# Message-passing kernel: node table ahead of the radial rows, rows broadcast from DRAM in nine pieces, first pass without a barrier

## What is computed

```python
s_j = silu(x[src][:, 384:] @ W1 + b1) @ W3 + b3
rbf = sqrt(2 / R_CUT) * sin(n * pi * r / R_CUT) / r      # n = 1..20, one r for each edge
edge_basis = (rbf * cutoff(r)) @ W2 + b2                 # 384 wide
s1, s2, s3 = thirds of s_j * edge_basis
msg = [v_j * s1 + s3 * edge_attr, s2]                    # 512 wide
x = x + segment_sum(msg, dst)
# a second round: U, V, norms and a gate on x[src], summed by dst again
out = layernorm(x0 + x)
```

## Time and profile before

| | |
|---|---|
| median of three runs | 798.62 us |
| the profiled execution's own span, first to last instruction | 711.8 us |
| DVE busy | 537.0 us (75%) |
| PE busy | 505.8 us (71%) |
| ACT busy | 389.5 us (55%) |
| POOL busy | 370.2 us (52%) |
| DMA: moved, mean rate | 139.26 MB, 196 GB/s |
| first pair's product in the pass (L926) | 154.72 us |
| last pair's product | 549.95 us |

### The profile page before, as it was taken

One profiled execution on the slowest core, in us unless ns is written; L12 is line 12 of the kernel. 1 busy time (PEld: TensorE's weight loads), 2 busy tenths in 40 slices (PEclk: granted clock), 3 DMA queues, 4 the chain that ended last, 5 costly groups with the idle time before them and its releaser, 6 DMA issues.

```text
span 711.8 us, 13058 instructions
## 1 busy us (share of the span) xinstructions
PE 505.8 (71%) x4260; PEld 234.1 (33%) x4269; DVE 537.0 (75%) x1192; ACT 389.5 (55%) x713; POOL 370.2 (52%) x375
## 2 busy tenths in 40 slices
PE   0276430038888888888888888888888286689996
PEld 0232110013333333334433333333333153344443
DVE  8868861029999999999999999999999443354283
ACT  1054331046777777776776777777776364343200
POOL 5004440067777777777777777777773131025300
PEclk9975555559999999999999999999999688689999
DMA  8413777699888888898888888888884400000021
GB/s 277 166 21 99 199 229 222 183 256 306 269 269 272 269 275 270 267 275 268 269 273 269 270 271 271 270 270 269 273 271 149 160 3 0 1 0 1 2 89 56
DMA packets 54193, 139.26 MB, mean 196 GB/s; under 512 B 10366, under 2 KB 21850, under 8 KB 54124
## 3 DMA queue, kind: packets, MB, share of 16 engines
q0 software_dynamic: 25120, 102.91, 46.3%
q1 hardware_dynamic: 23132, 25.80, 12.8%
q10 hardware_dynamic: 5872, 9.68, 4.1%
HBM read 120.47 MB, written 17.54 MB: 194 GB/s over the span
## 4 chain that ended last, share of the span: by engine, by line
DVE 39%; PE 35%; DMA 8%; issue 8%; ACT 3%; SPq 2%; POOL 2%; DVEq 1%; ACTq 1%; POOLq 0%
PE psum L1192 11%; DVE side L929 10%; PE psum L1282 9%; DVE hot L920 5%; DMA part_rows<-side 5%; DVE side L926 4%; PE psum L1157 4%; DVE work L929 3%; DVE work L947 3%; PE psum L1186 3%; PE psum L1251 3%; DVE hot L911 2%; SPq L358 2%; DVE side L916 2%; DMA side<-node_table,src_c 2%
## 5 line engine op out<-in xcount | busy, mean ns | idle before, releaser
L486 POOL DMA_INDIRECT side<-node_table,src_c x234 | 224.4, 959 | 71.3 <-issue 60.4
L604 ACT ACTIVATE side<-key_no,less_key 128x320 bf16<-128x320 f32 x314 | 159.3, 557 | 30.7 <-SPq L384 28.9
L612 ACT ACTIVATE side<-side,one_f 128x640 bf16<-128x640 bf16 x157 | 128.1, 816 | 10.0 <-PE psum L1168 10.0
L1157 PE MATMUL psum<-w2s,radial 123*128 123x384 bf16 x314 | 78.7, 333 | 66.3 <-DVE side L929 43.5
L1186 PE MATMUL psum<-side,hot 128*32 128x512 f32 x468 | 123.1, 605 | 0.5 <-DVE side L929 0.5
L929 DVE TENSOR_TENSOR side<-side,psum 128x768 f32<-128x768 f32 x117 | 110.5, 945 | 0.0
L486 POOL DMA_INDIRECT work<-node_table,src_c x80 | 76.8, 960 | 60.6 <-SPq L384 36.5
L1192 PE MATMUL psum<-side,hot 128*32 128x128 f32 x1404 | 99.4, 277 | 0.0
L926 DVE TENSOR_TENSOR side<-side,psum 128x512 f32<-128x512 f32 x117 | 79.4, 678 | 1.3 <-DMA side<-node_table,src_c 1.3
L1168 PE MATMUL psum<-side 128*128 128x320 bf16 x314 | 70.3, 306 | 0.5 <-ACT side L612 0.5
L1192 PEld LDWEIGHTS psum<-side,hot 128*32 128x32 f32 x1404 | 68.0, 109 | 0.1
(11 more groups left out here) (202 smaller groups left out, 738.0 us busy)
## 6 DMA issues: line engine op xcount, KB each, us to landing
radial<-part_rows SPq DMA_DIRECT2D x36, 270.0 KB
part_rows<-side SPq DMA_DIRECT2D x6, 810.0 KB, 12.7
side<-node_table,src_c POOLq DMA_INDIRECT x234, 4.2
sum_rows<-stage SPq DMA_DIRECT2D x212, 16.0 KB
node_table<-work ACTq DMA_DIRECT2D x10, 320.0 KB, 7.6
sum_rows<-zeros_bf SPq DMA_DIRECT2D x1, 2688.0 KB, 18.8
side<-sum_rows ACTq DMA_DIRECT2D x10, 256.0 KB, 4.7
xw<-in_x ACTq DMA_DIRECT2D x1, 2304.0 KB
```

What stands on the lines that cost most here:

```text
L486: g.indirect_dma_start(out=rows[i % SLOT_PAIRS][:, j, :], out_offset=None, in_=node_table, in_offset=bass.IndirectOffsetOnAxis(ap=src_c[:, ...
L604: a.activation(key_off[:, b, j, :], key_no[:, :], ACT.Abs, bias=less_key[:, t:t + 1]).then_inc(L["key_off_made"], 1)
L612: a.activation(key_hot[:, b, :, :], key_off[:, b, :, :], ACT.Relu, bias=one_f[:, :], scale=-1.0).then_inc(L["key_hot_made"], 1)
L1157: last = mm(bank[2 * (i % 2) + j][:, 0:C3], radial[0:RROWS + 3, t * P:(t + 1) * P], w2s[:, :], start=True, stop=True)
```

## The change

- **Order.** x is loaded into an area of its own (`x_in`), the 128 scalar columns first. Sigmoid, filters and the node table come before the radial pieces; the table has four buffers (`TABLES`), and its ten DVE products stand between the edge-table steps. The split of W2 and the biases moves from DVE to POOL, the copies of the edge attributes to ACT.
- **Radial rows.** r and `coef` are stored in DRAM as f32, and each piece's 120 rows of either are read back by one transfer that repeats each chunk 20 times (`rc_piece`, 360 KB). `pick`, the bf16 parts and PE's spreading are gone. Nine pieces of 768 columns, three `wave` buffers, still two of parts. DVE subtracts for pieces 0 to 3, POOL for 4 to 8, after it has issued the gathers of pairs 0 to 7.
- **SP's order.** Parts of piece 0 are stored, then the zeros of `sum_rows` are written (2688 KB; before this was at the start), then piece 0 is loaded; pieces 1 to 8 are all stored, then all loaded (48 transfers), then x is loaded a second time into `xw` for the residual (2304 KB and a tail), and only then come the stores of the sums.
- **First pass.** `message_pass`, `sum_pass`, `key_pass`, `gather` and `store_sums` run once outside a loop, each engine behind its own waits and without `pass_go`; further passes stand behind an `If` that this data does not take. DVE starts its pass when all nine pieces are scaled. In `take_total` the wait is now for `L["stored"]` at `64 * (n - 1)`: the same condition.

```diff
-PIECES = 6
-PB = 3
+PIECES = 9
+WAVES = 3
+POOL_FROM = 4
+TABLES = 4
...
-            sp.wait_ge(S["dve_const"], 2)
-            sp.dma_start(sum_rows.rearrange("(p b r) c -> p b (r c)", p=P, b=ZB),
-                         zeros_bf[:, :].bitcast(F32).unsqueeze(1).to_broadcast((P, ZB, 256))).then_inc(S["sums_zeroed"], 16)
...
+            sp.wait_ge(S["ld_r"], 32)
+            sp.dma_start(rc_rows[0].rearrange("(g f) -> g f", f=GE), r_r).then_inc(S["r_stored"], 16)
...
+            def store_parts(i):
+                sp.wait_ge(S["lo_made"], i + 1)
+                sp.dma_start(part_rows[:, :, i * PC:(i + 1) * PC].rearrange("k p f -> p k f"), part[i % 2]
+                             ).then_inc(parts_stored[i % 2], 16)
...
+            sp.wait_ge(S["r_stored"], 16)
+            for i in range(2):
+                sp.dma_start(r_in[i], rc_piece(0, i)).then_inc(r_loaded[i], 16)
+            sp.wait_ge(S["rc_made"], 1)
+            sp.dma_start(rc_rows[1].rearrange("(g f) -> g f", f=GE), coef).then_inc(S["coef_stored"], 16)
...
-                sp.wait_ge(S["lo_made"], i + 1)
-                sp.dma_start(part_rows[:, :, i * PC:(i + 1) * PC].rearrange("k p f -> p k f"), part[:, i % 2, :, :]
-                             ).then_inc(parts_stored[i % 2], 16)
-                if i:
-                    load_stack(i - 1)
-            load_stack(PIECES - 1)
-            sp.wait_ge(S["ranges_set"], 1)
-            stored_reg = sp.alloc_register("sums_stored")
-            sp.reg_mov(stored_reg, 0)
+                store_parts(i)
+                if i == 0:
+                    sp.dma_start(sum_rows.rearrange("(p b r) c -> p b (r c)", p=P, b=ZB),
+                                 zeros_bf[:, :].bitcast(F32).unsqueeze(1).to_broadcast((P, ZB, 256))).then_inc(S["sums_zeroed"], 16)
+                    load_stack(0)
+            for i in range(1, PIECES):
+                load_stack(i)
...
-                        sp.wait_ge(stored, sp.snap(stored_reg))
-                        sp.sem_inc(S["stores_seen"], 1)
+                        sp.wait_ge(L["stored"], 64 * n)
...
+            sp.dma_start(xw[:, 0:NFULL, :], x[0:NFULL * P, :].rearrange("(w p) f -> p w f", p=P)).then_inc(S["ld_x"], 16)
+            sp.wait_ge(S["x_pads"], 2)
+            sp.dma_start(xw[0:NTAIL, NFULL, :], x[NFULL * P:N, :]).then_inc(S["ld_x"], 16)
+            store_sums()
...
+            pool.wait_ge(S["edges_taken"], 3)
+            for b in range(TABLES):
+                pool.wait_ge(table_stored[b], 16 * through(NW, b, TABLES))
+            for i in range(SLOT_PAIRS):
+                gather(i)
+            for i in range(POOL_FROM, PIECES):
+                wv, pt = wave[i % WAVES], part[i % 2]
                 pool.wait_ge(S["hi_made"], i + 1)
-                g.tensor_tensor(wave[:, b, :], wave[:, b, :], part[:, b, 0, :], ALU.subtract).then_inc(S["wave_less_hi"], 1)
+                pool.wait_ge(S["lo_made"], POOL_FROM)
+                g.tensor_tensor(wv, wv, pt[:, 0, :], ALU.subtract).then_inc(S["wave_less_hi"], 1)
                 pool.wait_ge(S["mid_made"], i + 1)
-                g.tensor_tensor(part[:, b, 2, :], wave[:, b, :], part[:, b, 1, :], ALU.subtract).then_inc(S["lo_made"], 1)
...
+                g.tensor_tensor(pt[:, 2, :], wv, pt[:, 1, :], ALU.subtract).then_inc(S["lo_made"], 1)
+            for i in range(SLOT_PAIRS, PAIRS):
+                gather(i)
+            with more_passes(pool), pool.Fori(0, EXTRA) as r:
...
+            act.wait_ge(S["x_pads"], 1)
+            load_x(C3, D, S["ld_s"])
+            for to, from_ in ((w1[:, :], W1), (b1c[:, :], b1.rearrange("(p a) -> p a", a=1)), (w3[:, :], W3)):
+                a.dma_start(to, from_).then_inc(S["ld_table_weights"], 16)
+            load_x(0, C3, S["ld_v"])
...
+                       bank[(2, 3, 4)[c]][:, 0:NCOL].rearrange("p (j g) -> p j g", j=TJ)).then_inc(S["attr_taken"], 1)
 
             def take_filter(w):
-                b = w % 2
+                b = w % TABLES
                 act.wait_ge(S["filter_made"], w + 1)
-                if w >= 2:
-                    act.wait_ge(table_stored[b], 16 * (w // 2))
-                    act.wait_ge(S["table_vec_made"], w - 1)
-                a.copy(first_filter[:, b, :], bank[6 + b][:, 0:C]).then_inc(S["filter_taken"], 1)
-                a.copy(table_out[:, b, C3:TW], bank[6 + b][:, C:C3]).then_inc(S["table_rest_made"], 1)
+                if w >= TABLES:
+                    act.wait_ge(table_stored[b], 16 * (w // TABLES))
+                a.copy(table_out[:, b, C3:TW], filter_bank(w)[:, C:C3]).then_inc(S["table_rest_made"], 1)
 
             def store_table(w):
                 act.wait_ge(S["table_vec_made"], w + 1)
                 act.wait_ge(S["table_rest_made"], w + 1)
-                a.dma_start(node_table[w * P:(w + 1) * P, :], table_out[:, w % 2, :]).then_inc(table_stored[w % 2], 16)
...
+
+            def sine(i):
+                act.wait_ge(S["turn_made"], i + 1)
+                a.activation(wave[i % WAVES], wave[i % WAVES], ACT.Sin, scale=TWO_PI).then_inc(S["sin_done"], 1)
+
+            def high_part(i):
+                act.wait_ge(S["wave_scaled"], i + 1)
+                if i >= 2:
+                    act.wait_ge(parts_stored[i % 2], 16 * (i // 2))
+                a.copy(part[i % 2][:, 0, :], wave[i % WAVES]).then_inc(S["hi_made"], 1)
+
+            def middle_part(i):
                 act.wait_ge(S["wave_less_hi"], i + 1)
-                a.copy(part[:, i % 2, 1, :], wave[:, i % 2, :]).then_inc(S["mid_made"], 1)
-
-            for i in range(PIECES + 1):
-                b = i % 2
-                if i + 1 < PIECES:
-                    load_piece(i + 1, 0)
+                a.copy(part[i % 2][:, 1, :], wave[i % WAVES]).then_inc(S["mid_made"], 1)
+
+            for i in range(PIECES + 2):
                 if i >= 2:
-                    middle(i - 2)
-                    for w in (2 * i - 4, 2 * i - 3):
-                        if w < NW:
...
+            act.wait_ge(S["dve_const"], 7)
             act.wait_ge(S["tables_made"], 4)
 
             def key_offsets(i):
@@ -612,9 +600,6 @@
...
+            def turns(i):
+                wv = wave[i % WAVES]
+                dve.wait_ge(r_loaded[i % 2], 16 * (i // 2 + 1))
+                if i >= WAVES:
+                    dve.wait_ge(S["lo_made"], i - WAVES + 1)
+                v.tensor_scalar(wv, r_in[i % 2], harmonic[:, :], None, ALU.mult).then_inc(S["turn_begun"], 1)
+                dve.wait_ge(S["turn_begun"], i + 1)
+                v.tensor_scalar(nearest, wv, MAGIC, MAGIC, ALU.add, ALU.subtract).then_inc(S["turn_near"], 1)
+
+            def remainder(i):
+                wv = wave[i % WAVES]
...
+                dve.wait_ge(coef_loaded[i % 2], 16 * (i // 2 + 1))
+                v.tensor_tensor(wv, wv, coef_in[i % 2], ALU.mult).then_inc(S["wave_scaled"], 1)
+
+            def less_high(i):
+                wv = wave[i % WAVES]
+                dve.wait_ge(S["hi_made"], i + 1)
+                v.tensor_tensor(wv, wv, part[i % 2][:, 0, :], ALU.subtract).then_inc(S["wave_less_hi"], 1)
+
+            def low_part(i):
+                dve.wait_ge(S["mid_made"], i + 1)
+                v.tensor_tensor(part[i % 2][:, 2, :], wave[i % WAVES], part[i % 2][:, 1, :], ALU.subtract
+                                ).then_inc(S["lo_made"], 1)
+
             for i in range(PIECES + 1):
...
-
-            def messages(i):
+                    turns(i)
+                if 2 <= i < POOL_FROM + 2:
+                    less_high(i - 2)
+                if i < PIECES:
+                    remainder(i)
+                if 2 <= i < POOL_FROM + 2:
+                    low_part(i - 2)
+                if i:
+                    scaled(i - 1)
+                if i == 1:
+                    dve.wait_ge(S["uv_turned"], 1)
+                    v.tensor_copy(uT, bank[6][:, 0:C]).then_inc(S["uv_taken"], 1)
+                elif i == 2:
+                    dve.wait_ge(S["uv_made"], 1)
+                    v.tensor_copy(u_uv[:, 1, :], bank[7][:, 0:C]).then_inc(S["uv_set"], 1)
+
...
+            message_pass()
...
+            def sum_pass():
...
+            sum_pass()
+            with more_passes(pe), pe.Fori(0, EXTRA) as r:
+                pe.wait_ge(L["counts_taken"], NG)
...
```

586 lines of the change are left out of this document (273 added, 313 removed).

## The result

The changed kernel takes 826.92 us in the median of four runs (822.58 to 834.95), beside 798.18 us (796.58 to 803.75) for the kernel before: a ratio of 1.0339, interval 1.0286 to 1.0392. It is slower, by 28.7 us between the medians. The ratio leaves out one run, of 834.95 us, that counts as slow; over the other three the difference is 27.2 us. The forecast was 814.0 us with a range of 780 to 836, and slower was its likeliest case.

A forecast was written before the change was run, and what follows sets the result against it. It took DVE at 2.52 us a pair, with POOL at 2.5, to leave the pass no slack. Span 711.8 + 14 (later end) + 1 (restart) = 727 us; with 87 us carried over, 814 us, range 780 to 836.

The forecast's parts named there:

- The mechanism: Near pair 13: first sums queue behind SP's loads and x, `take_total` waits, a hole of 25 to 50 us on four engines.
- The way from ACT to the rest: At pair 13: its keys wait behind `take_total` on ACT, then PE's count, DVE's one-hots and POOL's slots, so the pass stops.
- Set-up to the first piece: Before the pieces: DVE begins its first piece at 46 us, bounds 40 and 52; before 45.62.
- The pieces: Nine-piece set-up: first low part near 58 us, `high_part(3)` at 94, last low part at 125, bounds 110 and 136.
- a rival: Piece set-up: broadcast loads and DVE stalled beside POOL push the low part to 136 us or later; 825 to 840, chance 0.08.
- Start of the pass: First pass: pair 2's product at 128 us against 161.39, 33 us gained, bounds 20 and 48.
- The loads and what stands behind them: SP's queue from 125 us: 48 loads 49 us, x 7, sums some 3, beside gathers of 26; landing 184 to 210.
- The landing of the first sums: First group's store at 202 us; pair 13 near 203.5 against 189.53 before, so the pass ends 14 us later.
- The 87 us: Difference between the profiled span and the median time of the kernel before, carried over unchanged to the forecast time.
- The pass: Main loop over pairs: no slack at 2.52 us a pair; unrolling costed at 0, at best -12 us.
- (a): Likeliest case: loads go into the pass and hold ACT; end 5 to 31 us later, 804 to 830, likeliest 814; chance 0.52.
- (c): Faster: first sums reach DRAM before ACT needs them at 156 us, or nearly; 766, or 770 to 790; chance 0.17.

The follow-up runs named there:

- e4: Changed kernel with SP loading only pieces 1 to 3 before the sums, 30 loads and x's second load on ACT's queue in the key pass; 716.46 us, ratio 1.002.
- e9: As e4, but SP loads piece 1 alone before the sums and 42 loads are on ACT's queue from pair 6; 791.9 us, ratio 0.9804.
- e6: Changed kernel with the five loads of U, V, Wu1, bu1 and Wu2 on SP behind the stores of pieces 1 to 3; 754.21 us, ratio 1.0535.
- e8: Changed kernel with piece 0's loads moved behind the store of piece 3 and the zeros behind that of piece 6 on SP; 820.39 us, ratio 1.0182.
- a0: Changed kernel, nothing edited, on a chip where the kernel before takes 715.5 us; 753.33 us, ratio 1.0541.
- e10: As e7, but the weight loads behind the stores of pieces 0 to 2 and DVE's two copies in steps 6 and 7; 685.59 us, ratio 0.9561.
- e2: Changed kernel with the zeros of sum_rows written early, ahead of the pieces; 752.22 us, ratio 1.0494.
- b0: Kernel before, nothing edited, profiled a second time; 721.69 us, span 719.9.
- e7: e8 and e9 together on the changed kernel, with the five weight loads on SP behind the stores of pieces 4 to 6; 780.73 us, ratio 0.9651.

## Why the prediction was right, and where it was not

**The mechanism was right.** Slower came from where it was forecast: SP reaches the 48 loads and x only after the pieces, the first sums are behind them, `take_total` of the third group waits, and with it everything. The hole, its cause and its waiters are those the prediction named; the way from ACT to the other engines is another, as said next. e4 and e9 show the cause by taking loads from ahead of the sums: with 48, 18 and 6 of them there the wait is 60.0, 23.2 and none. They move x with them and also spread the loads in time.

**The way from ACT to the rest: one step off.** The prediction let the keys of pair 13 stand behind `take_total`, and PE's count behind the keys. The waits shown first say that PE stopped one step earlier, at L1186, the sum of pair 12, and for ACT's copy at L611 itself. Group 4 begins with pair 12 and sums in the bank that group 2 used. PE may start on it when `take_total` has copied that bank out (`sums_taken`):

```python
def add_up(i):
    ...
    if first and n >= 2:
        pe.wait_ge(L["sums_taken"], n - 1)
```

DVE's one-hots of pair 14 need the sum of pair 12, so pair 13 still got its product, at 176.59 us. The keys of pair 13 would have held PE one step later. By the code, keys made ahead of the wait would not have helped; that was not run.

**Set-up to the first piece: right.** DVE's first turn (L864, the first scaling of r) stands at 44.94 us, forecast 46.

**The pieces: 12 us too early.** The first store of parts was forecast at 58 us and went out at 70.23. Two terms were missing. ACT's queue holds five weight loads ahead of the first sine, 44.2 to 54.6 us (the wait of 14.02 above), and the second pair of broadcast loads took 10.5 us to land. From that store on the steps held. To `high_part(3)` 36 us were forecast (58 to 94) and 35.7 measured (70.23 to 105.89), through exactly the named queue, if in other parts: 13.2 us to SP's next issue behind the zeros (forecast 19), 10.4 for stack 0 (6), 12 for the store of piece 1 (5), and 6 had been added for the traffic beside them. To the last low part 31 us were forecast and 31.5 measured (105.89 to 137.4), so the 11 us for two pieces were right in the mean (12.0 and 9.1). Sending the first store earlier alone returns nothing, though (e6): the queue behind it took up what the start gained. e8 shows that the order in the queue is what costs there.

**DVE beside POOL.** DVE's subtraction takes 0.96 us alone and 2.27 us beside POOL's, in the pieces that GpSimd splits (L871 in a0):

```profile
47.76 0.96 DVE L871 TENSOR_TENSOR xw<-xw,side 120x768 f32<-120x768 f32 x1
...
108.13 2.27 DVE L871 TENSOR_TENSOR xw<-xw,side 120x768 f32<-120x768 f32 x1
```

The prediction had seen this in the earlier trace rows and put it into a rival. It cost little: the chain that ended last runs through the store of a piece up to 122.4 us and from there through POOL's two subtractions. On that chain POOL's first one took 2.31 us twice and 1.67 once, so some 1.3 us went to it. The Trainium skill, "SBUF — State Buffer", section "SBUF: two separate sides", says the two engines share a port pair that an operation on one can lock against the other; the trace agrees with 0.96 against 2.27 us.

**Start of the pass.** The third product (pair 2) came at 142.47 us, forecast 128, before 161.39: 19 us gained instead of 33. Of the miss of 14.5 us, 12.4 are the pieces': the last low part came at 137.4 for 125. In a0, where pairs are fast, the third product stands at 138.99.

**The loads and what stands behind them: 10 us too cheap.** This is the second term that was mis-sized. From the start of the loads to the landing of the first sums the prediction had 77 us (125 to 202); it was 87 (137.81 to 225). The SP timeline of the changed kernel, cut at 178 us:

```profile
137.81 41.07 SPq L329 DMA_DIRECT2D radial<-part_rows  x21
```

```profile
177.21 28.27 SPq L329 DMA_DIRECT2D radial<-part_rows  x28
```

Alone a load takes 1.0 us, as the earlier trace rows gave (18.5 us for twelve of 270 KB); beside the gathers 2.0. So the gathers did not run free of charge in the three tenths that the share of 0.70 left free. The 21 loads took 20 us more than alone, and the gathers moved 6.86 MB in the window from 140 to 178 us, which at the 332 GB/s of the earlier trace rows is 21 us (an estimate). The sum in series, the prediction's upper bound of 85 us, was the measured one within 2 us. The miss does not show where it arose. SP was through with issuing the 48 loads after 67.7 us, as forecast (67 of the 77 us), and the 10 us for x and the sums became 19.5: from 205.5 to 225 us the engines moved 4.3 MB, of which x is 2.56. Some 1.7 MB of loads were thus still in the queue behind SP's last issue (an estimate). The Trainium skill, "DMA: Bandwidth & Descriptors", section "Why a DMA increments its semaphore by 16 and not by 1", was weighed in the prediction for this: ten of sixteen engines for 20 rows, gathers and loads in series, 210 us instead of 202. Counted from where the loads began, its case came true and the choice between the bounds did not. On the ten engines the trace agrees, and closer than the 0.70 that the prediction took for agreement: from 180 to 204 us the share is 0.69, of which the loads' own queue has 62.2%, beside 62.5% for ten of sixteen, and the last gathers 6.4%. In e10 the shares add up as well, 84.8% for the gathers, 9.9% for ACT's queue with the loads and 3.9% for SP's with the sums (140 to 240 us). There the loads come one every three pairs and fit into what the gathers leave.

**The landing of the first sums: 225 instead of 202.** The two misses are 13 (start of the loads, 137.81 for 125) and 10 us. The first product behind the hole was forecast at 203.5 us and stands at 228.28. It is that of pair 14, the 15th, and not that of pair 13. Set against pair 14 of before, 191.73, instead of 189.53, the same hole costs 2.2 us less; the restart, 3.2 us from landing to product instead of 1.5, costs 1.7 us more. The two nearly cancel. PE restarts at the lower of its two clock levels (1.2 GHz, granted clock 0.50 from 225 to 229 us, after 50 us of waiting), and a sum's first two matmuls take 1.07 us instead of 0.62.

**The number: in part luck.** With its two misses of 23 us the forecast shift of 15 us becomes 38, and 37.4 us is what the medians show on a chip like that of the profile (a0). There the shift is outside the likeliest case's own 5 to 31 us and stands at the very edge of the whole range, 836 - 798.6 = 37.4. On the chip of the timed runs the median moved by 28.7 us only, because slower pairs, which the prediction did not know of, took up part of the wait. That 826.92 lies well inside the range is owed to this.

**The 87 us: a wrong reading.** The prediction carried them over as time outside the span. They were the distance between two chips: the profiled execution was one of some 713.6 us. It did no harm to the sum, since only a difference was added. But the pass's pace of 2.52 us a pair did not hold where the times were taken.

**The pass: right.** Unrolling was costed at 0. e2 has DVE busy 286.99 of 300 us in the unrolled pass, b0 287.14 in the loop, and from the 15th product to the end of the span a0 and b0 agree within 0.4 us. (The prediction's "at best -12 us" took the idle 4% over 300 us; over the 396 us of the pass it is some 17. Nothing hangs on it.)

**Rivals.** (a) came true at its upper end: its shift was nearly twice the forecast, and 826.9 lies inside its own range of 804 to 830. On a chip like that of the profile it was two and a half times the forecast and lay beyond that range. (c), faster, was excluded at pair 13 as it said: landing at 225, where 188 was the point of decision. Its condition can be had, though. e10 meets it, not by faster loads but by sending them one by one and from another queue.

## What to carry to other kernels

A transfer that is moved from ahead of a barrier to behind it has not gone away: list what stands behind it in the same queue, and give the first result that must leave the core a queue of its own or the first place. When loads and gathers meet as a burst, add their times in series; spread over the work, one to every few steps, they cost little (4 us in e4 and e10, by the last section). A store that waits for the one before it to land is as slow as that landing, and loads in its queue lengthen it. A second profile of the same kernel can be 8 us off the first: compare medians. Look at the measured time of the very execution that was profiled before reading a difference between its span and the timed runs as anything.

## What the hardware showed that was not expected

**The delay of a signal differs between chips.** The same kernel before takes 716 us on three chips and 798 to 806 us where the others were timed. Each chip was seen in one stretch of time only, so whether this belongs to the chip or to the time is open. The profiles of the four kernels taken on the slower kind (the changed kernel, e7, e8, e9) all have waits named "remote" where the others wait for PE's sums; on the others such waits are missing or single. The waits of e9, 130 to 260 us, beside e10's for the same pass:

```profile
ACT stage L608 <- remote: 26.9, 12, 2.9
DVE hot L928 <- remote: 26.3, 27, 2.0
POOL side L461 <- remote: 20.7, 19, 1.6
```

```profile
ACT stage L609 <- PE psum L1216: 26.4, 16, 1.8
```

The operations take the same time on both, 0.68 us for the first product and 277 to 279 ns for the matmul that ends a pair. What differs is the wait for PE's signal, 0.9 us each time at DVE and POOL (59.8 us over 66 waits, 46.3 over 50, in the changed kernel; in a0 DVE waits there 13.1 us over 40, 0.3 each). Where DVE's one-hots wait between 300 and 500 us, they start 1.17 to 1.18 us after the end of the sum on PE that they wait for, in a0, b0, e4 and e10 alike; in the changed kernel, e8 and e9 it is 2.1 to 2.9 us, with medians of 2.42, 2.50 and 2.72. That is 1.2 to 1.5 us more from the same end to the same start. A pair takes 3.04 us in the changed kernel and 3.09 in e8 instead of 2.52, and over 157 pairs that is 81 to 88 us. This is about the 87 us. The kernel before was not profiled on the slower kind, so for it this is inferred and not shown; and why the signal is late there stays open.

**ACT's loads cost more on that kind.** From the 15th product to the end of the span, e4 and e10 with the loads in ACT's stream take 523.0 us, a0 without them 519.2. On the fourth chip e9 and e7 take 612.9 and 612.3 us, e8 without them 596.6: 16 us against 4. A pair takes 3.16 us in e9 and e7 and 3.09 in e8, which is 10 of the 16 over 142 pairs. That the issues, 0.75 us each, lie on the path more often where the pass waits for signals is a guess; it was not taken apart further.
